# Decoder layer on one core: the triangle of the decay factors moved from TensorE to GpSimd, with a new order of steps

## The chip, the core and the metric

The kernel runs on one core of a Trainium2 chip. A core has five engines with instruction queues of their own: TensorE (PE; its weight loads are shown apart as PEld), VectorE (DVE), ScalarE (ACT), GpSimd (POOL) and SyncE (SP), which here only issues transfers. They work side by side and wait for one another by semaphores. The metric is device microseconds of one execution, and lower is better.

## The reference, cut to what matters

There are 32 sequences of 128 rows of width 256. Each goes through a gated delta-rule attention block with a mixture of experts (called a here up to the attention's output, and b for the experts), then a cross attention, then a routed feed-forward block (both c), with layer norms between. What the change touches is in the first of them:

```python
g = -jnp.exp(A_log) * jax.nn.softplus(a + dt_bias)
def step(S, inp):
    qt, kt, vt, gt, bt = inp
    S = S * jnp.exp(gt)[..., None, None]
    kv = jnp.einsum('bhk,bhkv->bhv', kt, S)
    delta = (vt - kv) * bt[..., None]
    S = S + jnp.einsum('bhk,bhv->bhkv', kt, delta)
    o = jnp.einsum('bhk,bhkv->bhv', qt, S)
```

The kernel computes the 128 steps of that recurrence at once. For each of 8 heads it needs a 128x128 matrix of decay factors, exp(sum of g over the rows after p up to f), which counts only for p up to f and must be zero in the other triangle. It is multiplied with k·k and with q·k, and a triangular system is solved from the first product.

## The kernel before

The weights stay in SBUF. A software pipeline runs over the 32 sequences: one trip of it does part a of sequence n, part b of n-1 or n-2 and part c of n-2 or so, and the tables in `ORDER` give, for each engine, the steps of one trip in the order in which that engine's queue gets them ("@1" means of one sequence earlier than the step's part has by default). `run` writes the trips out one after another. Nothing else sets the order, so each engine does its steps strictly in the table's order, and each step begins with its own `wait_ge` lines.

The steps named below:

- `a_xT`, `a_qkv0` to `a_qkv3`, `a_z0`, `a_z1`: TensorE products of the first norm's output with the projection weights; ACT copies each of the four qkv groups out and scales the last tap of the convolution (`a_qkv`, five instructions). `a_conv..`: the other taps on DVE. `a_mix..`: SiLU on ACT.
- `a_ss`, `a_st`: sums of squares of q and k, and their transposition; `a_ss` on DVE writes `sse`. `a_sc` on POOL makes the scales from it.
- `a_dec0`, `a_dec1` (function `exponents`, four heads each): on TensorE first a bf16 product of `ident_bf` with `below_bf`, which puts -1e30 where f < p, then a float32 product of `later` with `gseg` on top of it in the same PSUM bank. ACT takes exp of the bank into `decay`, so that the wrong triangle becomes zero.
- `a_kk`, `a_qk`: k·k and q·k on TensorE, into banks A1 and A2. `a_lower` and `a_score` on DVE multiply them by `decay` (into `kkT`, `scoreT`).
- `a_init` on DVE begins the solution of the triangular system: four `diag` products, a transposition, the first `zblk` and `xblk`. `a_la00`, `a_lb00` and so on up to `a_la31`, `a_lb31`: levels of block inversion, each 16 small 32x32 products on TensorE (`level_a`, `level_b`) and one or two DVE instructions.
- `b_oT`, `b_w`: transposition of the attention's output (TensorE, copied by ACT) and its projection. `b_hid` on DVE adds the residual, `b_sum`/`b_rs` its mean square (ACT, POOL), `b_x2` on DVE the second norm, `b_x2T` its transposition (TensorE, ACT), `b_router` and `b_gu0` to `b_gu3` the experts' first products.
- `b_cT`, `b_v`, `b_mask`: the context's transposition, its values, its mask.
- `c_h`, `c_lg`, `c_c0`, `c_c1`, `c_wT`, `c_spread`, `c_pj0`, `c_pj1`: TensorE steps of the feed-forward block. `c_sum3`, `c_y3`: its residual and norm on DVE. `c_y2b` on POOL: two additions of 128x256.

## Time and profile before

| | |
|---|---|
| time, median of 3 runs | 2329.41 us (2327.68 to 2330.34) |
| time of the profiled execution | 2329.89 us |
| its span, first to last instruction | 2327.9 us |
| TensorE busy | 2219.2 us, 95% |
| VectorE busy | 1678.1 us, 72% |
| ScalarE busy | 1404.4 us, 60% |
| GpSimd busy | 768.9 us, 33% |
| mean granted TensorE clock | 0.984 |

A busy share is the time in which at least one instruction of the engine ran. Matmuls overlap, so the time that one really takes up on TensorE is the distance from its start to the start of the next. In the chain of work that ended last, TensorE has 55% of the span, VectorE 22%, ScalarE 18%.

### The profile page before, as it was taken

What the parts mean: (1) busy time and instruction counts of PE and PEld (TensorE: products, weight loads), DVE (VectorE), ACT (ScalarE), POOL (GpSimd) and SP (SyncE); (2) the same over time, 40 slices, a digit from 0 to 9 for tenths busy, and PEclk for the clock granted to TensorE, in tenths of its full rate; (3) what the DMA queues carried; (4) which work ended last, traced back from release to release, by engine and by line L of the source; (5) the groups of instructions that cost most, each with busy time, mean ns of one, the idle gap of its engine ahead of it and who ended that gap; (6) DMA issues with size and microseconds to landing.
All of it is one profiled execution on the core that took longest, in us unless ns stands there. A gap on an engine that the chain in (4) does not pass through costs nothing.

```text
span 2327.9 us, 82936 instructions
## 1 busy us (share of the span) xinstructions
PE 2219.2 (95%) x33994; PEld 1901.7 (82%) x34026; DVE 1678.1 (72%) x5322; ACT 1404.4 (60%) x4326; POOL 768.9 (33%) x1771
## 2 busy tenths in 40 slices
PE   5899999999999999999999999999999999999986
PEld 4788888888888888888888888888888888888875
DVE  4577777777777777777777777777777777777753
ACT  3576555776555776555776555776555776555742
POOL 2332324333324332324332324333323333324321
PEclk8899999999999999999999999999999999999997
DMA  6000000000000000000000000000000000000000
GB/s 221 7 2 10 9 10 9 9 2 10 10 9 9 9 2 9 10 9 9 9 2 9 10 10 9 9 2 10 9 10 9 9 2 9 10 9 9 7 4 3
DMA packets 25065, 30.75 MB, mean 13 GB/s; under 512 B 8529, under 2 KB 21857, under 8 KB 23921
## 3 DMA queue, kind: packets, MB, share of 16 engines
q1 hardware_dynamic: 24688, 25.46, 3.3%
q8 instruction: 270, 4.42, 0.8%
q14 instruction: 107, 0.87, 0.1%
HBM read 21.25 MB, written 4.19 MB: 11 GB/s over the span
## 4 chain that ended last, share of the span: by engine, by line
PE 55%; DVE 22%; ACT 18%; issue 4%; POOL 1%; DVEq 0%; POOLq 0%
PE bank_b L644 10%; PE bank_a L460 6%; PE bank_b L736 5%; PE bank_b L652 5%; DVE acc L1010 4%; PE bank_a L542 4%; DVE diag L1046 3%; PE bank_b L673 3%; DVE y1p L1140 3%; DVE u L1087 3%; PE bank_a L581 3%; PE bank_a L572 3%; ACT prob L923 2%; ACT acc L814 2%; PE bank_a L532 2%
## 5 line engine op out<-in xcount | busy, mean ns | idle before, releaser
L1010 DVE SCALAR_TENSOR_TENSOR acc<-ypad,convw,acc 128x128 f32<-128x128 f32 x1536 | 432.2, 349 | 73.0 <-ACT acc L814 72.7
L460 PEld LDWEIGHTS bank_a<-xnT,wqkvz 128*128 128x128 f32 x2048 | 242.6, 195 | 43.3 <-DVE u L1087 42.8
L460 PE MATMUL bank_a<-xnT,wqkvz 128*128 128x128 f32 x2048 | 258.9, 281 | 17.1 <-DVE u L1087 17.1
L911 ACT ACTIVATE y1T<-bank_b 128x256 f32<-128x256 f32 x32 | 12.3, 384 | 313.0 <-PE bank_b L666 313.0
L1417 POOL TENSOR_SCALAR lnv<-mv 128x1 f32<-128x1 f32 x128 | 31.1, 243 | 509.5 <-DVE mv L1101 506.9
L923 ACT ACTIVATE prob<-bank_b,nmax 128x128 f32<-128x128 f32 x512 | 179.7, 374 | 2.2 <-DVE nmax L1160 1.8
L814 ACT ACTIVATE acc<-bank_a,convw 128x128 f32<-128x128 f32 x512 | 149.4, 405 | 0.0
L1321 POOL TENSOR_TENSOR gate<-ba,dtb 128x8 f32<-128x8 f32 x32 | 6.5, 203 | 430.3 <-ACT ba L825 430.3
L1158 DVE TENSOR_REDUCE smax<-bank_b 128x4 f32<-128x512 f32 x128 | 87.8, 686 | 68.5 <-PE bank_b L683 68.5
L736 PEld LDWEIGHTS bank_b<-y2T,wc 128*128 128x128 f32 x1024 | 124.3, 195 | 14.4 <-issue 14.4
L903 ACT ACTIVATE prob<-bank_b 128x512 f32<-128x512 f32 x64 | 38.2, 597 | 160.1 <-PE bank_b L644 160.1
L542 PEld LDWEIGHTS bank_a<-ablk,xblk 32*32 32x32 f32 x8192 | 88.8, 107 | 55.2 <-issue 47.6
L644 PE MATMUL bank_b<-x2T,wg 128*128 128x128 f32 x1024 | 131.9, 282 | 0.0
L736 PE MATMUL bank_b<-y2T,wc 128*128 128x128 f32 x1024 | 130.0, 281 | 0.0
L532 PE MATMUL bank_a<-zblk,kkT 32*32 32x32 f32 x8192 | 114.1, 195 | 14.2 <-DVE zblk L1054 5.6
L652 PE MATMUL bank_b<-wd,prob 128*128 128x256 f32 x512 | 127.2, 392 | 0.0
L532 PEld LDWEIGHTS bank_a<-zblk,kkT 32*32 32x32 f32 x8192 | 93.8, 107 | 38.1 <-issue 33.4
L644 PE MATMUL bank_b<-x2T,wu 128*128 128x128 f32 x1024 | 124.8, 275 | 0.0
L759 PE MATMUL bank_b<-wp,prob 128*128 128x256 f32 x512 | 121.1, 380 | 1.1 <-DVE prob L1230 1.1
L644 PEld LDWEIGHTS bank_b<-x2T,wg 128*128 128x128 f32 x1024 | 120.7, 194 | 1.3
L1140 DVE SCALAR_TENSOR_TENSOR y1p<-bank_b,route,y1p 128x256 f32<-128x256 f32 x224 | 107.1, 478 | 20.2
L542 PE MATMUL bank_a<-ablk,xblk 32*32 32x32 f32 x8192 | 112.8, 195 | 8.1 <-issue 6.1
(244 smaller groups left out, 5845.3 us busy)
## 6 DMA issues: line engine op xcount, KB each, us to landing
xin<-in_x_dram SPq DMA_DIRECT2D x32, 128.0 KB, 2.1
cin<-in_ctx_dram SPq DMA_DIRECT2D x32, 128.0 KB, 2.1
out_dram<-yout SPq DMA_DIRECT2D x32, 128.0 KB, 2.9
wqkvz<-in_wqkvz_dram SPq DMA_DIRECT2D x6, 512.0 KB, 6.8
wout<-in_wout_dram SPq DMA_DIRECT2D x1, 1024.0 KB, 9.8
...
```

Of the source, the lines that this page charges most:

```text
L460: last = mm(A[bank][:, b * P:(b + 1) * P], wqkvz[:, c, o:o + P], xnT[:, c, :], start=(c == 0), stop=(c == KC - 1))
L532: last = mm(A_LEVEL[half][r, BLK * h:BLK * (h + 1)], kkT[r, h, r], zblk[r, h, :], start=True, stop=True)
L542: last = mm(A_LEVEL[half][r, BLK * h:BLK * (h + 1)], xblk[r, h, :], ablk[r, h, :], start=True, stop=True)
L644: last = mm(Bk[bank][:, b * P:(b + 1) * P], w[:, c, o:o + P], x2T[:, c, :], start=(c == 0), stop=(c == KC - 1))
L652: mm(Bk[DOWN[e]][:, D * (b % 2):D * (b % 2) + D], act_[:, e, :], wd[:, e, :], start=True, stop=True)\
L736: last = mm(Bk[2 + half][:, b * P:(b + 1) * P], wc[:, c, o:o + P], y2T[:, c, :], start=(c == 0), stop=(c == KC - 1))
L759: last = mm(Bk[2][:, 0:D], gcw[:, b, :], wp[:, b, :], start=(b == 0), stop=(b == 7))
L814: fn(acc[:, c, :], A[bank][:, b * P:(b + 1) * P], ACT.Copy, scale=convw[:, c, TAPS - 1:TAPS])\
L923: last = fn(prob[:, j, b, :], Bk[j][:, b * P:(b + 1) * P], ACT.Exp, scale=HD ** -0.5, bias=nmax[:, 4 * j + b:4 * j + b + 1], accum_out=esu ...
L1010: stt(acc[:, c, :], ypad[:, c, k:k + P], convw[:, c, k:k + 1], acc[:, c, :], ALU.mult, ALU.add).then_inc(conv.sem, 1)
L1140: stt(y1p[:, :], Bk[DOWN[e]][:, D * (b % 2):D * (b % 2) + D], route[:, e:e + 1], y1p[:, :] if e else xh[:, :], ALU.mult, ALU.add).then_inc ...
L1158: nc.vector.tensor_reduce(smax[:, 4 * b:4 * b + 4], quad(Bk[b]), AX_X, ALU.max).then_inc(smax_ok.sem, 1)
```

## The change

The bf16 product in `exponents` is dropped, with its two operands and the constant `below`. ACT now signals `decay_raw` when an exponential is written, and a new step on POOL, `mask` (`a_dm0`, `a_dm1`), waits for it, multiplies the four heads' 128x512 of `decay` in place by the 0/1 matrix `upto`, and signals `decay_ok`, for which `a_lower` and TensorE wait as before. All four tables of `ORDER` are new. The diff, with the tables cut to the places shown further below:

```diff
-for _name, _width in (("ident", P), ("upto", P), ("later", P), ("below", P),
+for _name, _width in (("ident", P), ("upto", P), ("later", P),
...
-    put("below", (f < p) * -1e30)
...
-       "c_wT a_ss c_spread a_st a_kk a_dec1 c_pj0 b_oT0 c_pj1 b_oT1 b_w0 b_w1 a_la00 a_la01 b_cT a_qk b_v "
-       "a_lb00 a_lb01 b_x2T".split(),
+       "c_wT a_dec0 c_spread a_dec1 c_pj0 c_pj1 a_kk b_oT0 b_oT1 b_w0 b_w1 a_la00 a_qk b_cT a_la01 a_lb00 "
+       "b_v b_x2T a_lb01".split(),
...
-        ident_bf = sb("ident_bf", [P, P], BF16)
-        below_bf = sb("below_bf", [P, 4 * P], BF16)
...
+        decay_raw = sig("decay_raw", 2)
...
-        PREP = 7
+        PREP = 5
...
-                mm(A[bank][:, :], ident_bf[:, :], below_bf[:, :], start=True, stop=False)
-                mm(A[bank][:, :], con("later"), heads(gseg, half), start=False, stop=True).then_inc(decay_ps.sem, 1)
+                mm(A[bank][:, :], con("later"), heads(gseg, half), start=True, stop=True).then_inc(decay_ps.sem, 1)
...
-                fn(heads(decay, half), quad(A[(0, 3)[half]]), ACT.Exp).then_inc(decay_ok.sem, 1)
+                fn(heads(decay, half), quad(A[(0, 3)[half]]), ACT.Exp).then_inc(decay_raw.sem, 1)
...
-            nc.vector.tensor_copy(ident_bf[:, :], ident).then_inc(prep.sem, 1)
-            nc.vector.tensor_copy(quad(below_bf), con("below").unsqueeze(1).to_broadcast([P, 4, P])).then_inc(prep.sem, 1)
...
+            def mask(n, half):
+                pool.wait_ge(*decay_raw(n, 1 + half))
+                tt(heads(decay, half), heads(decay, half), con("upto").unsqueeze(1).to_broadcast([P, 4, P]), ALU.mult)\
+                    .then_inc(decay_ok.sem, 1)
```

Four places of the new order follow; the line numbers of the kernel after are up to five lower than those before for the same statement.

TensorE, from `c_lg` to the projections, before:

```order
L742 MATMUL bank_b<-w,hT 128x16
L507 MATMUL bank_a<-below_bf,ident_bf 128x512
L508 MATMUL bank_a<-gseg,const 128x512
L736 MATMUL bank_b<-y2T,wc 128x128 x8
L746 MATMUL bank_b<-const,onehot 16x128
L484 MATMUL bank_a<-scoreT,ones 32x256 x4
L753 MATMUL bank_b<-wT,spread_bf 128x128 x8
L490 MATMUL bank_a<-const,scoreT 128x128 x2
L515 MATMUL bank_a<-mixed 128x128 x4
L507 MATMUL bank_a<-below_bf,ident_bf 128x512
L508 MATMUL bank_a<-gseg,const 128x512
L759 MATMUL bank_b<-wp,prob 128x256 x4
```

The same place after:

```order
L739 MATMUL bank_b<-w,hT 128x16
L733 MATMUL bank_b<-y2T,wc 128x128 x8
L488 MATMUL bank_a<-const,scoreT 128x128 x2
L733 MATMUL bank_b<-y2T,wc 128x128 x8
L743 MATMUL bank_b<-const,onehot 16x128
L505 MATMUL bank_a<-gseg,const 128x512
L750 MATMUL bank_b<-wT,spread_bf 128x128 x8
L505 MATMUL bank_a<-gseg,const 128x512
L756 MATMUL bank_b<-wp,prob 128x256 x8
L512 MATMUL bank_a<-mixed 128x128 x4
L594 MATMUL bank_b<-const,u 128x128 x8
L602 MATMUL bank_b<-wout,prob 128x256 x8
```

The two bf16 products are gone, `a_ss` stands ahead of `c_lg`, and `a_kk` (L515, now L512) stands behind both `c_pj` (L756), with the transpositions `b_oT` (L594) together behind it.

TensorE, from the end of `b_w` to the experts, before:

```order
L605 MATMUL bank_b<-wout,prob 128x256 x8
L532 MATMUL bank_a<-zblk,kkT 32x32 x32
L612 MATMUL bank_b<-const,cin 128x128 x2
L522 MATMUL bank_a<-mixed 128x128 x4
L620 MATMUL bank_b<-wv,cT 128x256 x2
L542 MATMUL bank_a<-ablk,xblk 32x32 x32
L626 MATMUL bank_b<-const,x 128x128 x2
L532 MATMUL bank_a<-zblk,kkT 32x32 x32
L632 MATMUL bank_b<-wr,x2T 128x8 x2
L644 MATMUL bank_b<-x2T,wg 128x128 x8
```

The same place after:

```order
L602 MATMUL bank_b<-wout,prob 128x256 x8
L529 MATMUL bank_a<-zblk,kkT 32x32 x16
L519 MATMUL bank_a<-mixed 128x128 x4
L609 MATMUL bank_b<-const,cin 128x128 x2
L529 MATMUL bank_a<-zblk,kkT 32x32 x16
L539 MATMUL bank_a<-ablk,xblk 32x32 x16
L617 MATMUL bank_b<-wv,cT 128x256 x2
L623 MATMUL bank_b<-const,x 128x128 x2
L539 MATMUL bank_a<-ablk,xblk 32x32 x16
L529 MATMUL bank_a<-zblk,kkT 32x32 x16
L629 MATMUL bank_b<-wr,x2T 128x8 x2
L641 MATMUL bank_b<-x2T,wg 128x128 x8
```

The halves of a level are spread among other products, and of `a_la10` and `a_la11` only the first still stands ahead of the router.

ACT, at the exponentials, before (`decay` is written by the exponentials):

```order
L967 ACTIVATE wT<-bank_b 16x128
L840 ACTIVATE scoreT<-bank_a 128x256
L953 ACTIVATE prob<-bank_b,bc 128x128 x4
L963 ACTIVATE lg<-lg,lsm 128x16
L851 ACT_TABLE_LOAD
L851 ACTIVATE decay<-bank_a 128x512 x2
L883 ACTIVATE prob<-bank_b 128x512 x2
```

The same place after:

```order
L964 ACTIVATE wT<-bank_b 16x128
L950 ACTIVATE prob<-bank_b,bc 128x128 x4
L960 ACTIVATE lg<-lg,lsm 128x16
L848 ACT_TABLE_LOAD
L848 ACTIVATE decay<-bank_a 128x512 x2
L808 ACTIVATE ypad<-bank_a 128x512
L811 ACTIVATE acc<-bank_a,convw 128x128 x4
L880 ACTIVATE prob<-bank_b 128x512 x2
```

The copy of the last qkv group (L808, L811), which frees the bank that `a_kk` writes, now stands behind the exponentials.

POOL, from `c_sig` on, before:

```order
L1441 TENSOR_SCALAR lg<-lg 128x16
L1304 TENSOR_TENSOR rqk<-sse,nhalf 128x8
L1341 TENSOR_TENSOR krb<-gate,rqk 128x8
L1343 TENSOR_TENSOR ckk<-krb,rqk 128x8
L1344 TENSOR_TENSOR irk<-sse,rqk 128x8
L1347 TENSOR_TENSOR eyec<-const,ckk 128x256
L1349 TENSOR_TENSOR pairc<-const,ckk 128x256
L1437 TENSOR_TENSOR y2pb<-y,rows 128x256
L1437 TENSOR_TENSOR y2lb<-y,rows 128x256
```

The same place after:

```order
L1437 TENSOR_TENSOR y2pb<-y,rows 128x256
L1437 TENSOR_TENSOR y2lb<-y,rows 128x256
L1299 TENSOR_TENSOR rqk<-sse,nhalf 128x8
L1336 TENSOR_TENSOR krb<-gate,rqk 128x8
L1338 TENSOR_TENSOR ckk<-krb,rqk 128x8
L1339 TENSOR_TENSOR irk<-sse,rqk 128x8
L1342 TENSOR_TENSOR eyec<-const,ckk 128x256
L1344 TENSOR_TENSOR pairc<-const,ckk 128x256
L1360 TENSOR_TENSOR decay<-decay,const 128x512 x2
L1390 TENSOR_SCALAR madj<-m_u,const 128x128
```

The two additions went ahead of `a_sc`, and the two masks stand behind it.

## Rows read from the trace of the kernel before

**Rows 1.** Busy time by stretch: length; then busy us of each engine, clock, DMA

```profile
999.48:1069.71 70.23, 68.39 (x1063) 58.62 (x1063) 52.22 (x168) 43.65 (x136) 23.96 (x56) 1.00 0.03 8
```

**Rows 2.** Timeline, TensorE, one trip: start us, length, instruction, idle time before it

```profile
999.48 1.02 PE L508 MATMUL bank_a<-gseg,const 128*128 128x512 f32 x2
...
1002.07 0.60 PE L597 MATMUL bank_b<-const,u 128*128 128x128 f32 x4
1002.50 1.89 PE L759 MATMUL bank_b<-wp,prob 128*128 128x256 f32 x8
...
1004.67 3.62 PE L605 MATMUL bank_b<-wout,prob 128*128 128x256 f32 x16
1008.22 0.75 PE L532 MATMUL bank_a<-zblk,kkT 32*32 32x32 f32 x64
...
1010.48 1.13 PE L620 MATMUL bank_b<-wv,cT 128*128 128x256 f32 x4 [0.24 <-ACT cT L887]
...
1012.53 0.44 PE L626 MATMUL bank_b<-const,x 128*128 128x128 f32 x2
...
1014.27 0.18 PE L532 MATMUL bank_a<-zblk,kkT 32*32 32x32 f32 x1 [0.52 <-issue]
1014.38 0.61 PE L632 MATMUL bank_b<-wr,x2T 128*128 128x8 f32 x4
1014.85 2.03 PE L644 MATMUL bank_b<-x2T,wg 128*128 128x128 f32 x16
...
1057.41 2.05 PE L460 MATMUL bank_a<-xnT,wqkvz 128*128 128x128 f32 x16 [0.49 <-DVE u L1087]
...
1069.50 0.38 PE L507 MATMUL bank_a<-below_bf,ident_bf 128*128 128x512 bf16 x1
1069.71 1.02 PE L508 MATMUL bank_a<-gseg,const 128*128 128x512 f32 x2
```

**Rows 3.** Groups by line and shape: the mask product on TensorE

```profile
L507 PE MATMUL bank_a<-below_bf,ident_bf 128*128 128x512 bf16 x32 | 12.1, 379 | 0.0
```

**Rows 4.** Timeline, VectorE, the end of the same trip

```profile
1001.78 1.23 DVE L1027 TENSOR_TENSOR kkT<-bank_a,decay 128x1024 f32<-128x1024 f32 x1 [0.52 <-ACT decay L851]
...
1006.16 0.49 DVE L1054 TENSOR_TENSOR zblk<-ablk,eyec 128x128 f32<-128x128 f32 x2
...
1006.99 0.44 DVE L1236 SCALAR_TENSOR_TENSOR y3p<-bank_b,lsm,y2pb 128x256 f32<-128x256 f32 x1
...
1009.21 0.41 DVE L1094 TENSOR_TENSOR hmid<-xres,bank_b 128x256 f32<-128x256 f32 x1
...
1011.96 0.48 DVE L1117 SCALAR_TENSOR_TENSOR x<-hmid,st_b,lnrow 128x256 f32<-128x256 f32 x1
```

**Rows 5.** Timeline, ScalarE, the same trip

```profile
1000.59 1.09 ACT L851 ACTIVATE decay<-bank_a 128x512 f32<-128x512 f32 x2
1002.71 0.60 ACT L883 ACTIVATE prob<-bank_b 128x512 f32<-128x512 f32 x1 [1.03 <-PE bank_b L597]
...
1013.01 0.38 ACT L895 ACTIVATE x2T<-bank_b 128x256 f32<-128x256 f32 x1 [2.58 <-PE bank_b L626]
...
1061.01 1.14 ACT L814 ACTIVATE acc<-bank_a,convw 128x128 f32<-128x128 f32 x4
```

**Rows 6.** Timeline, GpSimd, the same trip

```profile
998.83 1.68 POOL L1304 TENSOR_TENSOR rqk<-sse,nhalf 128x8 f32<-128x8 f32 x1 [3.71 <-DVE sse L1015]
...
1008.42 0.19 POOL L1417 TENSOR_SCALAR lnv<-mv 128x1 f32<-128x1 f32 x1 [4.38 <-DVE mv L1101]
```

**Rows 7.** Groups by line and shape: GpSimd's wide instructions

```profile
L1360 POOL TENSOR_SCALAR gseg<-const,gate 128x128 f32<-128x128 f32 x128 | 96.4, 765 | 6.9 <-POOL gate L1357 6.9
...
L1437 POOL TENSOR_TENSOR y2lb<-y,rows 128x256 f32<-128x256 f32 x32 | 30.2, 945 | 0.0
...
L1347 POOL TENSOR_TENSOR eyec<-const,ckk 128x256 f32<-128x256 f32 x32 | 19.7, 614 | 0.7
```

**Rows 8.** One tile's instructions, VectorE: duration ns min/median/max, first and last start

```profile
L1046 DVE TENSOR_TENSOR diag<-kkT,ckk x128: 411/421/857, 38.8 to 2192.3; 32x256 f32<-32x256 f32 x128
```

More of the change, by code:

```diff
@@ L1457, in before_b @@
                 pool.wait_ge(w_b.sem, W_B)
-            steps = dict(a_x=a_x, a_ga=a_ga, a_sc=a_sc, a_g=a_g, a_rq=a_rq, a_osc0=lambda n: out_scale(n, 0),
+            steps = dict(a_x=a_x, a_ga=a_ga, a_sc=a_sc, a_g=a_g, a_rq=a_rq, a_dm0=lambda n: mask(n, 0), a_dm1=lambda n: mask(n, 1), a_osc0=lambda n: out_scale(n, 0),
                          a_osc1=lambda n: out_scale(n, 1), a_xr=a_xr, b_xh=b_xh, b_mask=b_mask, b_rs=b_rs, b_rd=b_rd,
```

18 lines of the change are left out of this document (9 added, 9 removed), and 10 rows, old and new, of tables (dve, pe).

## The prediction, made before the changed kernel was timed

> **What bounds the kernel now.** I read the busy times first, then the timeline of one trip on TensorE, then on the other engines the steps that TensorE waits for. The pipeline repeats every 70.23 us: that is the distance between two starts of the second half of `a_dec1` [rows 2], and one stretch of that length holds a whole trip [rows 1]. TensorE is busy in 68.39 of those 70.23 us at full clock, against 52.2 us for VectorE, 43.7 for ScalarE and 24.0 for GpSimd [rows 1]. So TensorE's own work sets the trip, and what is left are short waits at a few places. The largest I find [rows 2] are at `b_v` (0.24 us idle, for ACT's copy of the context), inside `a_la11` (0.52 us, named "issue", but its operands come from VectorE, which is at that time busy with `b_x2`), and at `a_qkv2` (0.49 us, for `core`). 32 trips make 2247 us of the span; the rest is filling and emptying the pipeline. A change is therefore worth 32 times what it does to one trip's TensorE stream, and work on other engines costs nothing until TensorE waits for it.
>
> **Part 1: the product removed.** A matmul takes TensorE's time from its start to the next start. The mask product starts at 1069.50 and the next at 1069.71, so it costs 0.21 us, though its own duration reads 0.379 [rows 2, 3]. There are two in a trip (the trace lists 32 of the 64; records can be missing), hence -0.43 us a trip and -13.8 us in all. Nothing hid this work: TensorE had no idle time around it.
>
> **Part 2: the mask on GpSimd.** No row shows a 128x512 product on GpSimd. The nearest rows are two-input products of half that size [rows 7]: `eyec` at 0.61 us, and `y2lb` at 0.95 us, of which a part is collision with VectorE. Doubled they give 1.23 and 1.89 us for one mask. The ends are further off: no less than 0.61 us (the half-size instruction itself, since more elements don't take less), and no more than four times a `gseg` instruction of 128x128, 4 x 0.765 = 3.06 us. I take 1.3 us, near the first, because `eyec` also reads one operand by broadcasting. GpSimd has the time: it is idle 4.38 us behind this place [rows 6]. The question is latency, because `a_lower` on VectorE and, behind it, `a_la00` on TensorE wait for it. That is answered with the new order in part 3.
>
> A mask queued on GpSimd also holds up what stands behind it there: `b_mask`, then the two small instructions of a norm (`c_ln2`) and those of `b_rs`. They are first needed by `c_y3`, some 5 us later, and by `b_x2`, so this costs nothing up to masks of about 3 us each.
>
> The two operands of the mask both lie in SBUF. Rows show that such pairs disturb each other: a `diag` product on VectorE takes 0.41 us alone and 0.857 at worst, and the slow ones are those which start while `y2lb` runs on GpSimd [rows 8, 7]. In the new order the masks fall beside `a_conv22`, four instructions that read two SBUF tensors each. I allow up to 0.7 us of delay there, on both engines; VectorE has it free, since its next step `c_sum3` waits for `c_pj1` anyway. The Trainium skill has a rule for this ("SBUF — State Buffer", Who interferes with whom): a VectorE instruction with two SBUF inputs and a GpSimd instruction that reads SBUF lock each other out for their whole length. The rows on `diag` agree with it. Taken strictly it speaks against the change, since four convolution taps could each make a mask wait; the rival on the mask below prices that from rows.
>
> **Part 3: the new order, walked along one trip.** Times are on the trace's clock, so a step seen at 1008.22 comes again at 1078.45. I follow TensorE from `a_qkv2`, before which the order on TensorE hardly differs. `a_core1` should end within 0.1 us of before: ACT puts one copy (about 0.5 us) behind `a_qkv0`, so that the taps start earlier, and VectorE does two more tap groups in front. So `a_qkv2` starts at about 1057.5, after 1057.41 [rows 2].
>
> - From `a_qkv2` to `a_la00` the old stream took 1078.45 - 1057.41 = 21.04 us [rows 2]. Without the two mask products it is 20.6 us.
> - `b_oT0` and `b_oT1` now follow each other with no `c_pj1` between. ACT begins its copy 0.64 us after the transposition starts and takes 0.60 [rows 2, 5], so `b_w0` can start 1.24 us after `b_oT0`; two transpositions take 2 x 0.43 = 0.86. A new wait of 0.38 us.
> - `a_ss` and `a_st` standing alone and `c_lg` close behind `c_h` (ACT needs a table load there) cost perhaps 0.2 us, an estimate.
> - So TensorE reaches `a_la00` at 1057.5 + 20.6 + 0.4 + 0.2 = 1078.7. Is `zblk` there? `a_kk` ends ahead of `b_oT`, the wait and `b_w` (3.55 us, 1004.67 to 1008.22): 1078.7 - 0.86 - 0.38 - 3.55 = 1073.9. `c_sum3` starts when `c_pj1` is done, 0.9 us earlier, and holds VectorE for about 1.15 us (its first instruction 0.44, rows 4, and two more for the statistics; an estimate). `a_lower` therefore starts at about 1074.3. Before it started at 1001.78 + 70.23 = 1072.0: the chain to the solver starts 2.3 us later than it did. The pair of `zblk` starts at 1006.16, its first half ends some 0.3 later, so from `a_lower` to there are 1006.45 - 1001.78 = 4.67 us [rows 4]. That gives 1079.0, a wait of 0.3 us for TensorE.
> - The masks: `a_sc` takes GpSimd 3.6 us from `rqk` on (`rqk` starts at 998.83, and `y2pb` behind `a_sc` follows at 1002.4) [rows 6] and starts near 1067, so the first mask starts at about 1070.8, after its exponential (the pair takes 1.09 us and starts at about 1070.3) [rows 5]. With 1.3 us each the second ends at 1073.4, before 1074.3. **The masks are hidden**, by `a_kk` and `c_sum3`; each may take up to 1.7 us.
> - `a_kk` also waits for ACT's copy of the last qkv group, now behind the exponentials: 1071.4 + 0.48 + 1.14 = 1073.0 [rows 5], just when TensorE arrives there. No wait, but no slack either.
> - `a_la00` at 1079.0 is 0.55 us behind the old kernel. The gain comes behind it. Before, from `a_la00` to `b_gu0` took 6.63 us (1008.22 to 1014.85), with both waits named above and `a_la10`, `a_la11` in front of the router. Now `b_hid` starts 5.2 us after `a_lower` (1001.78 to 1006.99), at 1079.5; before at 1079.44. From `b_hid` to `b_x2` were 2.75 us (1009.21 to 1011.96) with two level steps between; now one, so 2.6, `b_x2` at 1082.1. The transposition follows 0.57 later, ACT's copy 0.48 after that and takes 0.38 [rows 2, 4, 5], the router 0.1 later, `b_gu0` 0.47 behind it: 1084.1, and 1084.3 with `a_la10` squeezed in ahead of the router. The old kernel had 1085.08. That is -0.8 us, of which `a_la11`, still to be done behind `b_gu1`, takes 0.3.
>
> **The sum.** -0.43 (products) + 0.1 + 0.4 + 0.2 + 0.3 (new waits up to `a_la00`) - 1.1 (waits gone between `a_la00` and `b_gu2`) = about -0.5 us a trip. Behind `b_gu2` the orders agree closely and VectorE, 52 of 70 us busy, has no new wait. 32 x -0.5 = -16 us. Once, in the first trip, nothing hides the masks: about +2 us, against some 0.5 us of preparation saved. The profiled execution took 2329.9 us, 0.5 above the median; so the median goes from 2329.4 to about **2315 us**, -0.6%. The same walk with each estimate at its worse or better side gives -0.2 to -0.9 us a trip, 2302 to 2324.5.
>
> **The rivals.** (1) *Only the product counts*, the new order gives back as much as it takes: -0.43 a trip, 2317 us. It lies so near that I keep it with the forecast; what tells them apart is the idle time at `a_la11` and `b_v`.
>
> (2) *The chain of the mask paces the solver; slower.* The place is `a_lower`, the price is whatever the second mask ends behind 1074.3, since `a_la00` and, by `b_hid` and `b_x2`, the experts' products all hang on it. The trip breaks even when `a_lower` starts 0.5 us later, at 1074.8: masks of 2.0 us each. Doubled `y2lb` (1.89 us) is nearly there; four `gseg` (3.06 us) would end at 1076.9, +2.6 us, net +2.1 a trip or 2398 us. With masks of 1.9 us and 0.7 us lost beside `a_conv22`, `a_lower` starts at 1075.3, +0.5 us a trip net, 2346 us. For it: no slack is left on the chain, and ACT's copy also ends on the same point. Against it: `eyec`, which is the nearest in shape, and that GpSimd and VectorE have other work only in part of that time.
>
> (3) *No difference.* Waits that I set at nothing (the copy of the last qkv group ahead of `a_kk`, `a_core1`, `b_v` behind ACT's mean square) take 0.1 to 0.2 us each: -0.1 us a trip, 2326 us.
>
> **How the numbers follow.** Forecast with rival (1): 0.68. Rival (3): 0.15. Rival (2): 0.12. Better than -0.9 us a trip, because TensorE's waits at the end of the trip fall away wholly: 0.05. A measurement of this kernel can tell about 0.2%, 4.7 us. Faster by more than that: nearly all of the first, the last, and a small part of (3), 0.74. Within it: 0.14. Slower: 0.12. The range of 8 in 10 takes the forecast's own bounds and most of (3), and the near edge of (2): 2300 to 2334 us.
>
> **What the profile after would show.** A mask of 1.2 to 1.5 us on GpSimd, and VectorE's `kkT` idle, if at all, for `c_pj1` or `a_kk` and not for GpSimd's `decay`. A period of 69.7 us. TensorE with no idle time ahead of `a_la11`, a new short one at `b_w0` and at `a_la00`. If `kkT` waits for the mask by more than 0.5 us a trip, or `a_kk` for ACT's `acc`, I am wrong by that rival; if the period is 69.8 with waits of the old size, the order did nothing.

## The result: 0.6% slower

| | before | after |
|---|---|---|
| time, median | 2328.76 us (2327.68 to 2330.34) | 2344.52 us (2340.23 to 2346.03) |
| runs | 4 | 4 |
| span of the profiled execution | 2327.9 us | 2344.2 us |
| VectorE busy | 1678.1 us | 1726.7 us |
| GpSimd busy | 768.9 us | 861.2 us |

The ratio is 1.0064, with a 95% interval of 1.0047 to 1.0082. The forecast was 2315 us with a range of 2300 to 2334. The time lies outside it, on the other side of the kernel before, and near the 2346 us that rival (2) had for a late mask.

From the page of the kernel after: busy times, the chain of work that ended last, and the group of VectorE's convolution taps (busy us, mean ns of one, then idle time before them).

```profile
PE 2218.3 (95%) x33962; PEld 1890.8 (81%) x33962; DVE 1726.7 (74%) x5320; ACT 1402.3 (60%) x4326; POOL 861.2 (37%) x1835
...
PE 49%; DVE 32%; ACT 11%; issue 5%; POOL 2%; DVEq 0%; POOLq 0%
...
L1007 DVE SCALAR_TENSOR_TENSOR acc<-ypad,convw,acc 128x128 f32<-128x128 f32 x1536 | 491.1, 387 | 25.6 <-ACT acc L811 25.5
```

TensorE lost 0.9 us of busy time and VectorE gained 48.6, although the change gives VectorE no instruction of size. In the chain, VectorE's share rose from 22% to 32% and TensorE's fell from 55% to 49%.

**Where the 16.3 us of span are.** One group splits the span at two points: TensorE's `c_s`, the first step of the last stage, which comes once in a trip. The row gives the start of its first matmul in the first trip that has it, and of its last matmul in the last. First of the kernel before, then of the kernel after:

```profile
L683 PE MATMUL bank_b<-kT,qT x1024: 270/270/575, 128.6 to 2288.7; 32*128 32x128 f32 x171
```

```profile
L680 PE MATMUL bank_b<-kT,qT x1024: 270/270/372, 135.6 to 2304.8; 32*128 32x128 f32 x171
```

The filling of the pipeline took 135.6 instead of 128.6 us, +7.0. From there to the last matmul of the last `c_s`, which is 31 distances and that step itself, it took 2169.2 instead of 2160.1, +9.1. The rest (39.4 against 39.2) is +0.2. So a bit under half was lost once, at the start, and the rest in the trips.

**A common trip, not any trip.** The distances between the starts of `c_s` are not equal. In the kernel before, 13 of the 31 are 69.53 us, and the others go up to 70.76; the one that the prediction walked through [rows 1, 2] has 70.23. After, the most frequent one is 69.97. The first 30 distances together (the last is shorter, since no new sequence begins in it) went from 2095.3 to 2105.2 us, +0.33 us on the mean of one. In the text below a step's place is its start behind the last `c_s`, in a trip of the most frequent length. TensorE in such a trip of the kernel before (start us, length, instruction, idle time before it); it answers to [rows 2]:

```profile
478.06 1.17 PE L683 MATMUL bank_b<-kT,qT 32*128 32x128 f32 x32
...
519.39 0.75 PE L532 MATMUL bank_a<-zblk,kkT 32*32 32x32 f32 x64
...
521.65 1.13 PE L620 MATMUL bank_b<-wv,cT 128*128 128x256 f32 x4 [0.25 <-ACT cT L887]
...
525.33 2.03 PE L644 MATMUL bank_b<-x2T,wg 128*128 128x128 f32 x16
...
547.60 1.17 PE L683 MATMUL bank_b<-kT,qT 32*128 32x128 f32 x32
```

And of the kernel after (the next `c_s` starts at 696.27):

```profile
626.31 1.17 PE L680 MATMUL bank_b<-kT,qT 32*128 32x128 f32 x32
...
662.20 1.05 PE L512 MATMUL bank_a<-mixed 128*128 128x128 f32 x8
663.09 1.04 PE L594 MATMUL bank_b<-const,u 128*128 128x128 f32 x8
664.37 3.72 PE L602 MATMUL bank_b<-wout,prob 128*128 128x256 f32 x16 [0.25 <-ACT prob L880]
668.53 0.45 PE L529 MATMUL bank_a<-zblk,kkT 32*32 32x32 f32 x32 [0.44 <-DVE zblk L1051]
...
673.70 1.47 PE L641 MATMUL bank_b<-x2T,wg 128*128 128x128 f32 x11
```

`a_la00` starts 42.22 us behind `c_s`, before 41.33. `b_gu0` starts at 47.39, before 47.27. So from `a_la00` to `b_gu0` are 5.17 us, before 5.94. The new waits stand where they were forecast, 0.25 us at `b_w0` and 0.44 at `a_la00`.

The masks themselves, as one line's answer (duration ns min/median/max, first and last start; then who idled for them):

```profile
L1360 POOL TENSOR_TENSOR decay<-decay,const x64: 1262/1274/1367, 37.1 to 2205.7; 128x512 f32<-128x512 f32 x64
...
  DVE kkT L1024: 8.5, 2
```

A mask takes 1.27 us, as forecast (1.3). And `kkT` waited for one only twice, 8.5 us in all; those are the first two items. In 30 trips nobody waits for a mask. What happens there is on VectorE, in the same trip as above. The taps are shown one by one, then `c_sum3`'s first instruction, `a_lower`, `zblk`:

```profile
659.77 0.35 DVE L1007 SCALAR_TENSOR_TENSOR acc<-ypad,convw,acc 128x128 f32<-128x128 f32 x1
...
661.32 1.35 DVE L1007 SCALAR_TENSOR_TENSOR acc<-ypad,convw,acc 128x128 f32<-128x128 f32 x1
...
662.60 0.45 DVE L1007 SCALAR_TENSOR_TENSOR acc<-ypad,convw,acc 128x128 f32<-128x128 f32 x1
662.98 0.47 DVE L1233 SCALAR_TENSOR_TENSOR y3p<-bank_b,lsm,y2pb 128x256 f32<-128x256 f32 x1
...
664.15 1.22 DVE L1024 TENSOR_TENSOR kkT<-bank_a,decay 128x1024 f32<-128x1024 f32 x1
...
668.09 0.49 DVE L1051 TENSOR_TENSOR zblk<-ablk,eyec 128x128 f32<-128x128 f32 x2
```

GpSimd at that time:

```profile
659.98 2.54 POOL L1360 TENSOR_TENSOR decay<-decay,const 128x512 f32<-128x512 f32 x2 [0.40 <-ACT decay L848]
662.52 0.65 POOL L1390 TENSOR_SCALAR madj<-m_u,const 128x128 f32<-128x128 uint8 x1
```

The four taps of `a_conv22` start 0.21 us ahead of the masks. The first takes 0.35 us, the next two 1.36 and 1.35, the last 0.45; together 3.28 us, where four taps alone take 1.13. The two in the middle each last until a mask has ended. It is the same in 30 trips: 60 of the 1536 taps took over 1 us, two in each. `c_sum3` follows without idle time, then `a_lower`, the solver's chain and TensorE's `a_la00`. The slowest of all 1536 taps took 1371 ns after and 458 ns before.

### The profile page after: what moved, and what is told of

The parts are those of the page before. It is cut to its first block, busy times and chain, and to the rows that moved or that the text cites. A ratio compares the mean times of both kernels' runs of the same rounds, so it can differ in the third digit from the quotient of the medians.

```text
span 2344.2 us, 82902 instructions
## 1 busy us (share of the span) xinstructions
PE 2218.3 (95%) x33962; PEld 1890.8 (81%) x33962; DVE 1726.7 (74%) x5320; ACT 1402.3 (60%) x4326; POOL 861.2 (37%) x1835
## 3 DMA queue, kind: packets, MB, share of 16 engines
HBM read 21.19 MB, written 4.19 MB: 11 GB/s over the span
## 4 chain that ended last, share of the span: by engine, by line
PE 49%; DVE 32%; ACT 11%; issue 5%; POOL 2%; DVEq 0%; POOLq 0%
PE bank_b L641 10%; DVE acc L1007 7%; DVE y1p L1137 5%; PE bank_a L458 5%; PE bank_b L733 5%; PE bank_b L670 3%; PE bank_a L578 3%; DVE u L1084 3%; PE bank_a L569 2%; PE bank_a L539 2%; DVE bn L1096 2%; DVE diag L1043 2%; ACT prob L920 2%; ACT acc L811 2%; DVE kkT L1024 2%
## 5 line engine op out<-in xcount | busy, mean ns | idle before, releaser
L1007 DVE SCALAR_TENSOR_TENSOR acc<-ypad,convw,acc 128x128 f32<-128x128 f32 x1536 | 491.1, 387 | 25.6 <-ACT acc L811 25.5
L1417 POOL TENSOR_SCALAR lnv<-mv 128x1 f32<-128x1 f32 x128 | 24.4, 190 | 401.7 <-DVE mv L1098 396.1
L811 ACT ACTIVATE acc<-bank_a,convw 128x128 f32<-128x128 f32 x512 | 148.7, 399 | 0.0
L529 PE MATMUL bank_a<-zblk,kkT 32*32 32x32 f32 x8192 | 120.1, 195 | 26.3 <-DVE zblk L1051 19.3
L602 PE MATMUL bank_b<-wout,prob 128*128 128x256 f32 x512 | 119.1, 386 | 8.0 <-ACT prob L880 8.0
L641 PEld LDWEIGHTS bank_b<-x2T,wu 128*128 128x128 f32 x1024 | 119.6, 192 | 0.0
L756 PEld LDWEIGHTS bank_b<-wp,prob 128*128 128x128 f32 x512 | 97.0, 190 | 27.5 <-DVE prob L1227 11.3
```

The source lines that it names most:

```text
L529: last = mm(A_LEVEL[half][r, BLK * h:BLK * (h + 1)], kkT[r, h, r], zblk[r, h, :], start=True, stop=True)
L602: last = mm(Bk[3][:, 0:D], coreT[:, h, :], wout[:, h, :], start=(h == 0), stop=(h == HV - 1))
L641: last = mm(Bk[bank][:, b * P:(b + 1) * P], w[:, c, o:o + P], x2T[:, c, :], start=(c == 0), stop=(c == KC - 1))
L756: last = mm(Bk[2][:, 0:D], gcw[:, b, :], wp[:, b, :], start=(b == 0), stop=(b == 7))
L811: fn(acc[:, c, :], A[bank][:, b * P:(b + 1) * P], ACT.Copy, scale=convw[:, c, TAPS - 1:TAPS])\
L1007: stt(acc[:, c, :], ypad[:, c, k:k + P], convw[:, c, k:k + 1], acc[:, c, :], ALU.mult, ALU.add).then_inc(conv.sem, 1)
```

## The experiments

All twelve in one table. "First c_s" is its first start, "common" the most frequent distance between two of them (neighbours within 0.03 us taken together), "30 trips" the first 30 distances added up (the last one varies between the kernels from 60.4 to 63.5 us); all three are from the profiled execution. e2, e3, e6 and e12 have neither the product nor the masks, so the triangle isn't applied in them. The ratio is against runs of the kernel before on the same chip, whose medians were 2328 to 2331 us.

| kernel | time us | ratio (95%) | first c_s | common | 30 trips |
|---|---|---|---|---|---|
| before | 2328.8 | 1 | 128.6 | 69.53 | 2095.3 |
| after | 2344.5 | 1.0064 (1.0047 to 1.0082) | 135.6 | 69.97 | 2105.2 |
| e1_order_only | 2337.6 | 1.0042 (1.0027 to 1.0057) | 138.0 | 69.75 | 2097.1 |
| e2_no_mask_new_order | 2325.4 | 0.9984 (0.9974 to 0.9994) | 133.2 | 69.40 | 2087.6 |
| e3_no_product_old_order | 2329.6 | 1.0002 (0.9992 to 1.0011) | 131.9 | 69.46 | 2095.6 |
| e4_conv22_early | 2334.9 | 1.0023 (1.0011 to 1.0036) | 135.4 | 69.64 | 2094.4 |
| e5_old_cT_first | 2331.6 | 1.0010 (1.0001 to 1.0020) | 133.0 | 69.53 | 2098.3 |
| e6_no_product_cT_first | 2333.2 | 1.0017 (1.0007 to 1.0028) | 129.5 | 69.46 | 2101.5 |
| e7_conv22_late | 2330.4 | 1.0000 (0.9988 to 1.0012) | 137.2 | 69.42 | 2086.5 |
| e8_act_first_trips | 2351.3 | 1.0087 (1.0070 to 1.0104) | 142.8 | 69.97 | 2106.3 |
| e9_dve_first_trips | 2334.4 | 1.0017 (1.0008 to 1.0026) | 135.0 | 69.43 | 2095.2 |
| e10_all_first_trips | 2331.9 | 1.0008 (0.9999 to 1.0017) | 137.0 | 69.43 | 2087.1 |
| e11_vector_masks_first | 2324.2 | 0.9972 (0.9959 to 0.9984) | 129.5 | 69.41 | 2088.9 |
| e12_no_mask_first_old | 2324.7 | 0.9972 (0.9960 to 0.9983) | 128.1 | 69.42 | 2087.3 |

### Taking the change apart

The change has three parts: the product goes, the mask comes, the order is new. Three kernels have each some of them.

The new order alone, in the kernel before, with the product kept and no mask. The edit puts the new `ORDER` in, without `a_dm0 a_dm1`:

```diff
-    pool="b_mask@2 b_rs@2 c_ln3@3 b_xh@2 ... c_sig a_sc c_y2b c_ln2 a_rq".split(),
+    pool="c_ln2@3 b_rs@2 b_xh@2 a_xr@1 ... c_sig c_y2b a_sc b_mask".split(),
```

> The kernel before with the changed kernel's order of steps: the bf16 mask product is still on TensorE, there is no mask on GpSimd. Theory 'lock' (the masks on GpSimd hold up a_conv22 on VectorE by 2.1 us and with it c_sum3, a_lower and a_la00): without them the common trip loses TensorE's wait at a_la00 of 0.6 us and gains two products of 0.21, so 69.97 + 0.43 - 0.6 = 69.8 us, about 2340 us. Theory 'order' (the new order makes a_lower late by itself, the masks cost nothing more): 69.97 + 0.43 = 70.4 us a trip, about 2357 us.

The kernel after without the masks, so with neither product nor mask:

```diff
-                fn(heads(decay, half), quad(A[(0, 3)[half]]), ACT.Exp).then_inc(decay_raw.sem, 1)
+                fn(heads(decay, half), quad(A[(0, 3)[half]]), ACT.Exp).then_inc(decay_ok.sem, 1)
-       "c_ln1 a_g c_rx c_sig c_y2b a_sc a_dm0 a_dm1 b_mask".split(),
+       "c_ln1 a_g c_rx c_sig c_y2b a_sc b_mask".split(),
```

> The changed kernel without the masks on GpSimd, so the triangle is not applied at all (the output is that of unmasked decay factors); ScalarE signals decay_ok itself. Theory 'lock': a_conv22 takes 1.1 us again instead of 3.3, a_lower starts some 1 us or more earlier against c_pj1, the wait at a_la00 (0.6 us) goes: 69.4 us a trip, about 2326 us. Theory 'order': 69.9 to 70.0, no more than 5 us below the changed kernel's 2344.

The kernel before without the product, in its old order:

```diff
-                mm(A[bank][:, :], ident_bf[:, :], below_bf[:, :], start=True, stop=False)
-                mm(A[bank][:, :], con("later"), heads(gseg, half), start=False, stop=True).then_inc(decay_ps.sem, 1)
+                mm(A[bank][:, :], con("later"), heads(gseg, half), start=True, stop=True).then_inc(decay_ps.sem, 1)
```

> The kernel before without the two bf16 mask products, no mask anywhere, old order (the triangle is not applied). It prices the removed work alone. If TensorE's stream is what counts: 69.53 - 0.43 = 69.10 us a trip, 2314 to 2316 us. If waits close up behind it (VectorE's chain is what counts there): less than half of that, above 2321 us.

Of the three, e1 and e2 came out at what theory 'lock' had, and e3 on the side of the second theory. The common trip: the order alone +0.22 us (69.53 to 69.75). The product taken out in the new order -0.35 (e1 to e2, 69.40). The masks put in +0.57 (e2 to the kernel after, 69.97). The product taken out in the old order only -0.07 (69.46), and nothing in the time: 1.0002. The forecast had put -0.43 for the product, about -0.1 for the order and nothing for the masks. In the new order the product gave nearly its due; the masks' price and the order's are what went wrong. And the product's value isn't a property of the product: it depends on the order around it.

The 30 trips added up say the same of the masks (+17.6 us) and of the product in the new order (-9.5), but not of the order: it costs 1.8 us in them and not 30 x 0.22, because the rarer trips of the old order are longer (up to 70.76 us, in e1 up to 70.27). Most of the time that e1 lost is in its filling (138.0 against 128.6).

### Why the product was worth nothing in the old order

TensorE in a common trip of e3 (the next `c_s` starts at 549.15):

```profile
479.70 0.50 PE L682 MATMUL bank_b<-kT,qT 32*128 32x128 f32 x8
...
523.21 1.13 PE L619 MATMUL bank_b<-wv,cT 128*128 128x256 f32 x4 [0.45 <-ACT cT L886]
...
525.26 0.44 PE L625 MATMUL bank_b<-const,x 128*128 128x128 f32 x2
...
526.88 2.03 PE L643 MATMUL bank_b<-x2T,wg 128*128 128x128 f32 x16
```

Behind the second half of `a_dec1` TensorE runs 0.28 us ahead of the kernel before, as far as the product in front of `b_v`. There the wait for ScalarE's `cT` is 0.45 us where it was 0.25, and `b_gu0` is at 47.18 against 47.27. My theory then was that ScalarE's order, `b_sum` in front of `b_cT`, was what gave the gain back (the wait at `b_v` in the kernel before is 0.25 us, not the 0.4 of the expectation below). Two kernels swap the two steps, in the kernel before and in e3:

```diff
-    act="b_oT0@2 b_oT1@2 a_mix2@1 b_sum@2 b_cT@2 b_x2T@2 b_sg0@2 ...
+    act="b_oT0@2 b_oT1@2 a_mix2@1 b_cT@2 b_sum@2 b_x2T@2 b_sg0@2 ...
```

> The kernel before with one swap on ScalarE: the copy of the context's transposition (b_cT) ahead of the mean square of b_sum, so that it no longer waits for b_hid. In the kernel before TensorE waits 0.4 us at b_v for that copy in every trip. Theory 'the wait at b_v is what stands between TensorE and VectorE's chain': the wait goes and the common trip falls from 69.53 to 69.1 to 69.2 us, about 2317 us. Theory 'the next wait comes late too' (b_x2T for b_x2, which hangs on b_hid as well): TensorE stops there instead, no more than 0.1 us a trip, 2326 us or more.

> The same swap, and the two bf16 mask products left out (the triangle is not applied, as in the second run). Without the swap leaving them out brought 0.08 of 0.43 us a trip. Theory 'b_v': with the swap the products are worth more, at least 0.28 us, common trip 68.8 to 68.9 us. Theory 'VectorE's chain': TensorE meets b_x2T or a level of the solver instead and the products are worth 0.1 us again, 69.3 to 69.4 us.

TensorE in a common trip of e6 (the next `c_s` starts at 829.76):

```profile
760.30 0.50 PE L682 MATMUL bank_b<-kT,qT 32*128 32x128 f32 x8
...
803.20 1.03 PE L619 MATMUL bank_b<-wv,cT 128*128 128x256 f32 x4
804.16 0.45 PE L541 MATMUL bank_a<-ablk,xblk 32*32 32x32 f32 x32
805.49 0.45 PE L541 MATMUL bank_a<-ablk,xblk 32*32 32x32 f32 x32 [0.87 <-issue]
...
807.49 2.03 PE L643 MATMUL bank_b<-x2T,wg 128*128 128x128 f32 x16
```

The wait at `b_v` is gone and `b_v` starts at 42.90 instead of 43.51. But then TensorE waits 0.87 us a step later, and `b_gu0` is at 47.19, where it was. The theory fell. The swap didn't shorten the common trip by more than a hundredth. What stands behind both waits is VectorE: `b_x2`, whose result the next transposition needs, starts at

```profile
805.30 0.48 DVE L1116 SCALAR_TENSOR_TENSOR x<-hmid,st_b,lnrow 128x256 f32<-128x256 f32 x1
```

45.00 us behind `c_s`, and at 45.07 in the kernel before, whatever TensorE does. Followed backwards, VectorE works from `kkT` to `b_x2` with hardly a gap, and `kkT` waits 0.52 us for ScalarE's `decay` [rows 4]. ScalarE's exponentials start at 33.70 in the kernel before and 33.63 in e3 (medians of 22 trips), since ScalarE first takes the router's exponential and a table load. That one hangs on the routing chain, which the first product shortened by 0.07. So the second product (0.21 us) stood beside a chain on ScalarE and VectorE on which the trip depended more. Of the first product's 0.21 us, 0.07 were left at that chain's start.

That is the common trip. Of the times of e3, e5 and e6 a part is TensorE's clock. In the kernel before and the kernel after, the granted clock stayed at 1.00 (2.4 GHz) in all the 30 trips; in e3 it fell to 0.50 (1.2 GHz) in two of them, in e5 in four and in e6 in nine, each time near `b_gu0`, behind the 32x32 products of the solver and short waits of TensorE. The first trip of e6, TensorE's instructions and then the clock from 177 to 180 us (behind the busy times, as in [rows 1]):

```profile
174.72 0.45 PE L541 MATMUL bank_a<-ablk,xblk 32*32 32x32 f32 x32 [0.84 <-issue]
...
176.26 0.69 PE L631 MATMUL bank_b<-wr,x2T 128*128 128x8 f32 x4
176.79 3.59 PE L643 MATMUL bank_b<-x2T,wg 128*128 128x128 f32 x16
...
177.00:180.00 3.00, 3.00 (x15) 3.00 (x16) 2.06 (x8) 0.00 (x0) 0.00 (x0) 0.50 0.00 0
```

`b_gu0` takes 3.59 us there and 2.03 in a common trip, and the trip 71.09 instead of 69.46. The two trips of e3 took 71.69 and 73.76; its other 28 have a mean of 69.65, against 69.84 for the 30 of the kernel before. So with the clock at 1.00 the product would have been worth some 0.2 us a trip in the old order, an estimate from one execution of each kernel: about half of the forecast, and not nothing.

The falls fit the times of e5 and e6, which are slower than the kernel before by 0.10% and 0.17% although their common trips are no longer. They go with the waits just before them: 0.87 us in every trip of e6 (nine falls), 0.65 in e5 (four), 0.25 and 0.15 in the kernel before (none); the two of e3 are in trips with a further wait of 0.43 and 0.77 us. Why the clock falls in one such trip and not in the next is open.

In the new order TensorE's `c_pj1` comes late enough that `c_sum3`, and with it the whole VectorE chain, waits for TensorE. There the same product was worth 0.35.

### The lock between the masks and the convolution taps

Two kernels change nothing but the place of `a_conv22` on VectorE. The first puts it in front of `c_gc0`, before the masks begin:

```diff
-       "... a_ss a_conv21 c_gc0 c_weight c_gc1 a_conv22 c_sum3 "
+       "... a_ss a_conv21 a_conv22 c_gc0 c_weight c_gc1 c_sum3 "
```

> The changed kernel with one step moved: a_conv22 on VectorE ahead of c_gc0 instead of behind c_gc1, so that it no longer runs beside the masks. Theory 'lock': c_gc0 starts about 0.3 us later (it had waited 0.74 us), c_sum3 no longer waits for the taps, a_lower starts up to 1 us earlier: 69.97 - 0.4 = 69.6 us a trip, about 2332 us. Theory 'order': within 3 us of the changed kernel's 2344, or slower by c_gc0's delay.

The second puts it behind the masks, between `a_lb01` and `a_conv30`:

```diff
-       "... a_ss a_conv21 c_gc0 c_weight c_gc1 a_conv22 c_sum3 "
-       "a_lower a_init b_hid a_la00 c_y3 b_x2 a_la01 a_lb00 b_v a_lb01 a_conv30 a_la10 a_conv31 b_top "
+       "... a_ss a_conv21 c_gc0 c_weight c_gc1 c_sum3 "
+       "a_lower a_init b_hid a_la00 c_y3 b_x2 a_la01 a_lb00 b_v a_lb01 a_conv22 a_conv30 a_la10 a_conv31 b_top "
```

> The changed kernel with a_conv22 moved on VectorE from beside the masks to behind a_lb01, 10 us later, where GpSimd is idle and nothing waits for it soon. Theory 'lock': all that the masks cost in the steady trip (0.56 us against the kernel without them) goes: 69.4 us a trip; the first two trips stay as slow as in the changed kernel, so 2327 to 2329 us. If the masks also cost by their own latency (a_lower waiting for decay_ok): 69.6 us or more.

In both, no tap is longer than 0.46 us. e4 gives back 0.33 us of the 0.57; what is left is that the second `c_gc` comes 1.1 us of taps later, and TensorE's `c_pj1` with it: the step behind it, `a_kk`, starts at 36.13 instead of 35.89. e7 gives back 0.55 and stands 0.02 above the kernel with no masks at all. A common trip of e7 (it begins at 415.24, the next at 484.64), VectorE's `c_sum3` and `a_lower`:

```profile
451.33 0.48 DVE L1233 SCALAR_TENSOR_TENSOR y3p<-bank_b,lsm,y2pb 128x256 f32<-128x256 f32 x1 [2.54 <-PE bank_b L756]
...
452.52 1.23 DVE L1024 TENSOR_TENSOR kkT<-bank_a,decay 128x1024 f32<-128x1024 f32 x1
```

its masks:

```profile
448.92 2.49 POOL L1360 TENSOR_TENSOR decay<-decay,const 128x512 f32<-128x512 f32 x2 [0.40 <-ACT decay L848]
```

and TensorE:

```profile
456.95 0.45 PE L529 MATMUL bank_a<-zblk,kkT 32*32 32x32 f32 x32
...
462.07 2.03 PE L641 MATMUL bank_b<-x2T,wg 128*128 128x128 f32 x16
```

VectorE now waits 2.54 us for `c_pj1`, and starts `c_sum3` at 36.09 instead of 36.67. The masks end at 36.17, and `a_lower` starts at 37.28: they are hidden, with 1.1 us to spare, as the prediction's walk had it. `a_la00` is at 41.71 with no wait and `b_gu0` at 46.83. In the steady trips, the whole of the masks' price was the lock.

The lock is in the kernel before as well, in another place: one of the four `diag` products [rows 8] took 0.86 us instead of 0.41 in each of 30 trips, behind `kkT`, where `y2lb` runs on GpSimd, and `y2lb` took 0.96 us and not the 0.73 that it takes in the kernel after. The new order took the additions away from there, and the four products fell from 2.15 us:

```profile
514.21 2.15 DVE L1046 TENSOR_TENSOR diag<-kkT,ckk 32x256 f32<-32x256 f32 x4
```

to 1.71:

```profile
665.41 1.71 DVE L1043 TENSOR_TENSOR diag<-kkT,ckk 32x256 f32<-32x256 f32 x4
```

That is a gain of 0.44 us which the new order had on VectorE's chain, and the masks beside `a_conv22` took more than that away again.

### The filling of the pipeline

e7 has a common trip 0.11 us shorter than the kernel before, and its 30 trips together are 8.8 us shorter. Its time is the same, since its first `c_s` comes 8.6 us later. I thought first of ScalarE, whose copy of the last qkv group now stands behind the exponentials. This kernel lets ScalarE walk its old order in the first two trips of the kernel after:

```diff
-                for name, lag in plan:
+                for name, lag in (early if trip <= 2 else plan):
-            run(steps, ORDER["act"], act, before_b)
+            run(steps, ORDER["act"], act, before_b, FIRST_ACT)
```

> The changed kernel with ScalarE's old order in trips 1 and 2 only. The changed order makes the first two intervals 8.6 us longer. Theory 'last qkv copy': that is TensorE waiting 2.8 us at a_kk in each of the two trips for the copy that stands behind the exponentials on ScalarE; the two intervals become 5 to 6 us shorter, 2338 to 2340 us. Theory 'taps': it is the longer way of VectorE through a_conv and a_core in trip 2 (waits of 3.7 us at a_qkv2): no more than 2 us shorter.

It made the filling 7.2 us longer (142.8) and left the trips as they were. Both theories fell. That it got so much longer suggests that the orders of the engines belong together; no run here shows by what. The same edit for VectorE, on e7 and for three trips, and then for TensorE, VectorE and ScalarE together for two trips:

```diff
+            run(steps, ORDER["dve"], dve, before_b, FIRST["dve"])
```

> e7_conv22_late (the changed kernel with VectorE's a_conv22 behind a_lb01) in whose first three trips VectorE walks the order of the kernel before, while every other engine and every later trip keeps the new order. Theory A: the longer fill of the new order (the first two distances between a_xn were 128.3 us in e7 and 118.1 in the kernel before) comes from VectorE's order alone: the two distances come to 118 to 121 us, the later trips stay at 69.43, and the time is 2320 to 2323. Theory B: TensorE's order makes the fill longer: the two distances stay at 126 to 130 and the time at 2328 to 2333.

```diff
+            run(steps, ORDER["pe"], pe, before_b, FIRST["pe"])
+            run(steps, ORDER["act"], act, before_b, FIRST["act"])
+            run(steps, ORDER["dve"], dve, before_b, FIRST["dve"])
```

> e7_conv22_late in whose first two trips TensorE, VectorE and ScalarE all walk the orders of the kernel before (with a_conv22 where that kernel has it); later trips as in e7. Theory A (the order of the first two trips is what makes the fill longer, whichever engine's): the first two distances come near the 118.1 us of the kernel before, up to 122 with the passage into the new order, the common trip stays at 69.43, and the time is 2320 to 2324, under the kernel before by 0.2 to 0.4%. Theory B (the fill is made longer behind the first two trips, by the first pass through the new order with all three stages in work): the two distances may come down, but the trips behind them give it back: the time stays at 2328 to 2333.

Neither helped: 135.0 (with one distance of 77.45 us at the passage into the new order) and 137.0. With all three old orders e10 differs from the kernel before, in these trips, by the masks, the missing product and GpSimd's own order. VectorE's `kkT` of the first and the second item tells the rest. The kernel before:

```profile
37.50 1.23 DVE L1027 TENSOR_TENSOR kkT<-bank_a,decay 128x1024 f32<-128x1024 f32 x1 [1.45 <-ACT decay L851]
...
95.73 1.22 DVE L1027 TENSOR_TENSOR kkT<-bank_a,decay 128x1024 f32<-128x1024 f32 x1 [1.46 <-ACT decay L851]
```

e10:

```profile
40.91 1.22 DVE L1028 TENSOR_TENSOR kkT<-bank_a,decay 128x1024 f32<-128x1024 f32 x1 [5.21 <-POOL decay L1364]
...
102.94 1.22 DVE L1028 TENSOR_TENSOR kkT<-bank_a,decay 128x1024 f32<-128x1024 f32 x1 [5.21 <-POOL decay L1364]
```

GpSimd at the first of them:

```profile
34.74 1.71 POOL L1303 TENSOR_TENSOR rqk<-sse,nhalf 128x8 f32<-128x8 f32 x1 [4.83 <-DVE sse L1016]
...
38.33 2.48 POOL L1364 TENSOR_TENSOR decay<-decay,const 128x512 f32<-128x512 f32 x2
```

In the filling nothing stands between the exponentials and `kkT`, and GpSimd comes to its masks only behind `a_sc` (`rqk` is its first instruction; the expectations below name `a_rq`, which is a slip). Two kernels check this, both made from e10. The first lets VectorE, which is idle there, do the masks of the first two items:

```diff
             def a_lower(n):
                 dve.wait_ge(*kk_ps(n))
+                for half in range(2 if n <= 2 else 0):
+                    dve.wait_ge(*decay_raw(n, 1 + half))
+                    tt(heads(decay, half), heads(decay, half), con("upto")..., ALU.mult).then_inc(decay_ok.sem, 1)
                 dve.wait_ge(*decay_ok(n))
             def mask(n, half):
+                if n <= 2:
+                    return
                 pool.wait_ge(*decay_raw(n, 1 + half))
```

> e10_all_first_trips in whose first two items VectorE, not GpSimd, does the two mask multiplications, directly ahead of a_lower's kkT, where it was idle (in e10 kkT followed 5.21 us of idle time on VectorE in each of the two, released by GpSimd's decay, against 1.46 in the kernel before). Theory A (in the fill the masks stand in the path: GpSimd comes to them only behind a_rq, and nothing else hides them): two VectorE multiplications of 128x512, about 0.7 us each by its other rows of that shape, end earlier than GpSimd's pair by some 2.5 us in each of the two trips; the first two distances come from 128.2 down to 121 to 124 us, the common trip stays at 69.43, and the time is 2323 to 2328. Theory B (the longer fill has to do with the passage into the new order): the distances stay near 128 and the time at 2330 to 2334.

The second has no masks at all (the edit of e2):

> e10_all_first_trips without GpSimd's two mask multiplications in any item, so the triangle isn't applied and ScalarE's exponentials release a_lower directly. Theory A: the first two distances come to those of the kernel before, 117 to 120 us (128.2 in e10), the common trip is 69.4, and the time is 2319 to 2324. Theory B: the distances stay above 124 as in e2_no_mask_new_order (124.4), and the time at 2325 to 2330.

The first `c_s` comes at 129.5 and 128.1 us instead of 137.0. In e11 the two items' `kkT` start at 37.54 and

```profile
96.61 1.22 DVE L1028 TENSOR_TENSOR kkT<-bank_a,decay 128x1024 f32<-128x1024 f32 x1
```

6.3 us ahead of e10, behind two VectorE multiplications of 0.69 us. So the masks on GpSimd cost some 7.5 to 9 us in the filling of e10; the times agree (ratio 1.0008 against 0.9972 twice, 8.4 us). A part of that is TensorE's clock. In the second item, TensorE of e11:

```profile
101.10 0.74 PE L533 MATMUL bank_a<-zblk,kkT 32*32 32x32 f32 x64 [0.99 <-DVE zblk L1059]
...
106.91 2.03 PE L645 MATMUL bank_b<-x2T,wg 128*128 128x128 f32 x16
```

and of e10, with the stretch in which the granted clock was 0.50 (length; busy us of TensorE, its weight loads, VectorE, ScalarE, GpSimd; then the clock):

```profile
107.31 1.08 PE L533 MATMUL bank_a<-zblk,kkT 32*32 32x32 f32 x64 [4.19 <-DVE zblk L1055]
...
114.42 2.03 PE L645 MATMUL bank_b<-x2T,wg 128*128 128x128 f32 x16
...
107.00:112.00 5.00, 4.68 (x78) 4.17 (x78) 3.47 (x12) 0.78 (x3) 1.84 (x4) 0.50 0.02 5
```

Behind the longer wait for `zblk` (4.19 us against 0.99) the clock was low, and from `a_la00` to `b_gu0` it took 7.11 us instead of 5.81. The 6.2 us by which e10 was behind at `a_la00` became 7.5 at `b_gu0`.

The masks are not all of it in the kernel after. Its `kkT` of the second item waited 4.26 us for the mask, yet e2, with the new order and no masks, also has its first `c_s` at 133.2, 5 us behind e12, which differs from it only by the old orders in the first two trips and the place of `a_conv22`. A single value of the first `c_s` is good to some 3 us only: e3, e5 and e6, whose orders are old but for one swap and which have no masks, have 131.9, 133.0 and 129.5. Read with that, the new order costs some 5 us in the filling (133.2 to 138.0 in the kernels that have it throughout; 128.1 to 133.0 in those with old orders and no masks on GpSimd). With the old orders the masks on GpSimd cost some 9 us more. That they cost anything on top of the new order (133.2 to 135.6, but 138.0 in e1 without masks) isn't shown. What in the new order makes the filling longer stays open.

e11 is also the version that comes out ahead of both kernels: 2324.17 us (2321.74 to 2327.99), ratio 0.9972 with an interval of 0.9959 to 0.9984. It has the product's work off TensorE, the masks beside nothing that they lock, and a filling as in the kernel before (129.5 against 128.6).

## Why the prediction was wrong, step by step

Three steps failed. The delay beside `a_conv22` was put at nothing for VectorE, and cost 0.57 us a trip. The waits gone between `a_la00` and `b_gu2` were put at 1.1 us, from a trip with a rare wait in it, and were 0.46. The filling was put at +2 us, and was +7.0.

**What bounds the kernel.** "TensorE's own work sets the trip" was read from 68.39 busy us of 70.23. But a busy share of 97% doesn't say that work taken away is time gained. e3 took 0.43 us of work away and the common trip fell by 0.07, since a chain over ScalarE and VectorE, from the router's exponential through `kkT` to `b_x2`, was about as long and had no slack. "Work on other engines costs nothing until TensorE waits for it" was true, and that point was nearer than the busy times showed.

**Part 1, the product (-0.43 forecast).** The work was sized right, and in the new order the trip got 0.35 of it. "Nothing hid this work: TensorE had no idle time around it" was right only there. In the old order, to which the prediction's sum added it, the other chain hid it: TensorE was 0.28 us ahead behind both products, and gave it back 11 to 13 us further on, at `b_v` and `b_x2T`. In the common trip the new order pays 0.22 us (e1) and gets 0.28 more out of the product; the forecast counted the product in full and took the order as a gain too.

**Part 2, the mask (1.3 us forecast, 1.27 measured).** Right in length, and right that nothing behind it on GpSimd suffered. Wrong in what it does to its neighbour: "up to 0.7 us of delay there" became 2.15 (3.28 against 1.13 for four taps), and "VectorE has it free" became 0.58 us of delay for `c_sum3` and all behind it. The first size came from rows in which one VectorE instruction met a GpSimd instruction of 0.95 us; two taps that each wait for a mask of 1.27 us lose 1.0 each. The slack I counted on, `c_sum3`'s wait for `c_pj1`, exists and is 2.54 us long in e7, where `a_conv22` stands elsewhere. Four locked taps take 3.28: 0.7 us more than there is, and 0.58 were measured. Without the lock they would have fitted with 1.4 to spare. The prediction never made that subtraction. The rule of the Trainium skill ("SBUF — State Buffer", Who interferes with whom) that was cited there agrees with these rows: each of the two taps that met a mask waited for the whole of it. I had followed it only for the masks' delay, and there the rows show next to none: the masks went from 1.27 to 1.31 us.

**Part 3, the walk.** From `a_qkv2` to `a_la00` I had 21.5 us and the trace shows 21.9 (20.32 to 42.22 behind `c_s`). `a_qkv2` is 0.03 late, forecast 0.1; the wait at `b_w0` is 0.25, forecast 0.38. `a_la00` came +0.9 instead of +0.55. That is the lock (without it, in e7, it came +0.4), less an error to the other side: the 4.67 us from `a_lower` to `zblk` had the slow `diag` product in them, which the new order did away with. From `a_la00` to `b_gu0` I had 5.3 us, and it is 5.17. **The old side was wrong by 0.69 us**: the 6.63 us from `a_la00` to `b_gu0` [rows 2] are those of one trip, with a wait of 0.52 us inside `a_la11` that the common trip hasn't (four of the 30 trips have one, of 0.23 to 0.52 us); there it is 5.94. "1.1 us of waits gone between `a_la00` and `b_gu2`" was 0.46 in truth (`b_gu2` starts at 51.83 us, before 51.39). The two terms, wrong by 0.64 and 0.35, carry the forecast of about -0.5 us to the +0.44 measured.

**Once, in the first trip (+2 forecast).** +7.0 us. Right that nothing hides the masks there (it said so, and the trace names GpSimd's `decay` twice), but it counted one item and not two, nothing of the new order (some 5 us by the runs, cause open), and nothing of the clock.

**The rivals.** Rival (2) had the right place (`a_lower` late, and with it `a_la00` and the experts' products), nearly the right time, and the wrong way: not masks of 1.9 us that come late, but masks of 1.27 that end in time and hold up VectorE's taps. It had a chance of 0.12 because the masks' length spoke against it; the lock needed no long mask. That the times agree (2346 and 2344.5) is luck: it put all of the loss into the trips, where 9 of 16 us are. Rival (1), the product alone at 2317, is out: e3 is at 2329.6, and e7, without the lock, at 2330.4. Rival (3) had the common trip of e7, 0.1 us less than before, but neither the lock nor the filling. The signs named at the end ruled out rival (2) as it stood, since `kkT` doesn't idle for the mask in a trip; none of them would have shown the taps. The period is 69.97 and not 69.7.
